# Graph layer and expert layer on one core: order of stored groups, earlier YTh, YTl and YL, and a last group finished by tiles

## The chip, the cores and the metric

The kernel runs on one core of one Trainium2 chip. The metric is device time in microseconds: the median over runs of the whole program. Each run is one launch.

## The reference

There are 12,500 nodes with 256 values each and 200,000 edges. Two layers follow each other, both with a residual:

```python
x = x + gnn(layernorm(x), src, dst, edge_weight, W, b)      # segment_sum((X @ W)[src] * w, dst) + b
x = x + ffn(layernorm(x)[None], Wr, br, W1, b1, W2, b2, gamma, beta)[0]

# ffn, with xn = layernorm(x), 8 experts, D = 256, F = 512
logits = mean(xn over nodes) @ Wr + br                      # one routing for all nodes
two experts with the largest weight, softmax over these two # only known when every node is done
h = gelu(xn @ W1[e] + b1[e]);  y[e] = h @ W2[e] + b2[e]
out = layer_norm(sum_e weight[e] * y[e] + xn) * gamma + beta
```

The routing needs the mean over all nodes, so the two experts are known only when the graph layer has ended.

## The kernel before, in words

The 98 tiles of 128 nodes are processed in 25 groups: group 0 has two tiles, the others four. Groups 0 to 7 (`AHEAD = 8`) are put through all eight experts during the graph layer, while TensorE has room, and their outputs are stored in DRAM (`y_d`); they are called stored groups here. Groups 8 to 24, the list `post` of 17 groups, are put through the two chosen experts in a last stage. The change lies in that last stage alone.

The last stage computes in split precision. An fp32 value is written as a rounded part and the rest: YTh and YTl for the turned input of a group, W1h and W1l, W2h and W2l for the weights, Hhi and Hlo for the hidden values. Three products replace one.

All engines run their instructions in the order in which the program writes them, and wait on semaphores. The loops of the last stage go over rounds `k` and steps `i` of 0 to 7 (`HID = 8`), a step being 128 of the 2 x 512 hidden columns:

- **TensorE**: round `k` does `up(k+1, i)`, then `down(k, i)`. `up` needs YTh (L1463) and YTl (L1466) of its group, and that Hhi of four steps earlier has been made (four PSUM banks). `down(k, i)` needs Hlo of that step; twelve products (L1494) of four tiles, and at the last step two bias matmuls (L1499).
- **ScalarE**: round `k` does `hidden(k, i)`, two Gelu passes (Ht, L878, and Hhi, L881); the results of TensorE's round `k - 1` come to it step by step. In between stand `high(k+1)` (YTh, L804) at step 3, and `normal2(n)` (XN, L812), which needs XL in SBUF: at step 4 for a stored group, at step 6 for group `k`.
- **VectorE**: round `k` does `low_h(k, i)` (Hlo, L1194), and in between `low(k+1)` (YTl, L1105) at step 4, and the finishing of group `post[k-2]`: `total` at steps 0 and 1 (add L1211, statistics L1219, aggregation L1222, variance L1225) and `give` at steps 3 and 4 (L1232, L1237). Where `k - 2` is a key of `pre_of`, a stored group is finished too, at steps 2, 5 and 7; such a round is called a doubled round.
- **GpSimd**: adds a bias to XN of stored groups (L576), adds beta to XL (L578), and raises the variance to the power -0.5 (ZR, L583) for each group.
- **SyncE** issues all DMAs of the stage in one order, `for n, g in enumerate(order)`: for a group of `post` first `load_yl(k+3)`, then it waits until the group is finished (`s_fin`), stores it, loads XL of the fourth group after it, and after a stored group the next stored outputs (YP).

`order` puts the stored groups between those of `post`: `pre_of` maps a place in `post` to the stored group that follows it. Before, the places are 1, 2, 4, 6, 8, 9, 11 and 13, so VectorE's doubled rounds are 3, 4, 6, 8, 10, 11, 13 and 15. VectorE's loop runs two rounds longer than TensorE's, and finishes the last two groups there.

Of the kernel before, what the change touches and what calls it, by code (L numbers as in the profile page):

```python
# [4 lines left out]
P = 128  # L5
NODES, D, F, E = 12500, 256, 512, 8
# [100 lines left out]
def gnn_ffn(nc, x, dflat, srct, dstt, wt, W, b, Wr, br, W1, b1t, W2, b2, gamma, beta, cst, iota_e, evt, out):  # L107
# [13 lines left out]
    with ctx:  # L121
# [5 lines left out]
        def sem(name):  # L127
            return ctx.enter_context(nc.semaphore(name))
# [122 lines left out]
        s_xbn, s_xag, s_xv, s_xy, s_xq, s_xs = sem("dve_x_stats"), sem("dve_x_aggr"), sem("dve_x_var"), sem("act_x_seed"), sem("dve_x_newton"), sem("act_x_scale")  # L251
# [109 lines left out]
        def _(e):  # L361
# [147 lines left out]
            e.wait_ge(s_w2l, 2)  # L509
            for a in range(2):  # L510
                load_y(a)
            k = 0
            for n, g in enumerate(order):
                m = len(tiles(g))
                if g >= AHEAD:
                    if k + 3 < len(post):
                        load_yl(k + 3)
                    k += 1
                e.wait_ge(s_fin, first_of[n] + m)
                top = NT - tiles(g)[0] - m  # L520
                if g == 0:
                    e.dma_start(out[top * P:(NT - 1) * P, :].rearrange("(t p) d -> p t d", p=P), Z[:, n % 3, 0:m - 1, :]).then_inc(out_st[n % 3], 16)
                    e.dma_start(out[(NT - 1) * P:NODES, :], Z[0:LAST, n % 3, m - 1, :]).then_inc(out_last, 16)
                else:
                    e.dma_start(out[top * P:(top + m) * P, :].rearrange("(t p) d -> p t d", p=P), Z[:, n % 3, 0:m, :]).then_inc(out_st[n % 3], 16)
                if n + 4 < NG:
                    load_x1(n + 4)
                if g + 2 < AHEAD:
                    load_y(g + 2)
            for k in range(3):  # L530
                e.wait_ge(out_st[k], 16 * ((NG - 1 - k) // 3 + 1))
            e.wait_ge(out_last, 16)

        @block.gpsimd
        def _(e):
# [50 lines left out]
            for n in range(NG):  # L586
                until = min(n + (2 if n + 1 < NG and order[n + 1] < AHEAD else 1), NG - 1)
                while added <= until:
                    add_rows(added)
                    added += 1  # L590
                rstd(n)

        @block.scalar
        def _(e):
# [168 lines left out]
            def seed_x(b):  # L763
                a, z = lots[b][0] * GT, min(lots[b][-1] * GT + GT, NT)
                e.wait_ge(s_xv, b + 1)
                e.activation(xy[:, a:z], xv[:, a:z], ACT.Abs_reciprocal_sqrt).then_inc(s_xy, 1)

            def scale_x(b):
                e.wait_ge(s_xq, 3 * b + 3)
# [114 lines left out]
            for k in range(len(post) + 1):  # L884
                for i in range(HID):
                    if k < len(post):
                        hidden(k, i)
                    if k == 0 and i in (2, 3):
                        high_w2(i - 2)
                    if i == 3 and 1 <= k and k + 1 < len(post):  # L890
                        high(k + 1)
                    if i == 1 and k == 1 or i == 4 and k - 1 in pre_of:
                        normal2(n)
                        n += 1
                    if i == 6 and 1 <= k < len(post):
                        normal2(n)
                        n += 1
            assert n == NG

        @block.vector  # L900
        def _(e):
# [45 lines left out]

            def x_newton(b):
                a, z = lots[b][0] * GT, min(lots[b][-1] * GT + GT, NT)
                e.wait_ge(s_xy, b + 1)  # L950
                e.tensor_tensor(out=xq[:, a:z], in0=xy[:, a:z], in1=xy[:, a:z], op=ALU.mult).then_inc(s_xq, 1)
                e.wait_ge(s_xq, 3 * b + 1)
                e.scalar_tensor_tensor(out=xq[:, a:z], in0=xq[:, a:z], scalar=-0.5, in1=xv[:, a:z], op0=ALU.mult, op1=ALU.mult).then_inc(s_xq, 1)
                e.wait_ge(s_xq, 3 * b + 2)
                e.scalar_tensor_tensor(out=xr[:, a:z], in0=xq[:, a:z], scalar=1.5, in1=xy[:, a:z], op0=ALU.add, op1=ALU.mult).then_inc(s_xq, 1)

            e.wait_ge(dst_in, 32)
            e.tensor_scalar(LOW[:, :], DST[:, :], P - 1, None, ALU.bitwise_and).then_inc(s_tab, 1)
# [282 lines left out]
                e.wait_ge(x1_st[k], 16 * ((NT - 1 - k) // 4 + 1))  # L1241
            for k in range(2):
                e.wait_ge(ye_st[k], 16 * (UNITS // 2))
            for k in range(len(post) + 2):
                n = place[post[k - 2]] if k >= 2 else None
                two = k - 2 in pre_of
                for i in range(HID):
                    if k < len(post):
                        low_h(k, i)
                    if k == 0 and i in (2, 4):  # L1250
                        low_w2(i // 2 - 1)
                    if k == 0 and i == 7:
# [10 lines left out]
                        give(n, slice(2, 4))  # L1263
                    if two and i == 5:
                        total(n + 1, None, slice(2, 4))
                    if i == 4 and 1 <= k and k + 1 < len(post):
                        low(k + 1)
                    if two and i == 7:
                        give(n + 1, slice(0, 4))

        @block.tensor
        def _(e):
# [280 lines left out]
```

## Time and profile before

| | |
|---|---|
| median of 3 runs | 2426.01 us (2422.8 to 2431.03) |
| profiled execution | 2431.56 us |
| its span | 2429.8 us |
| busy: TensorE, VectorE, ScalarE, GpSimd | 2240.1, 1025.5, 1184.3, 1618.5 us |
| mean granted clock of TensorE | 0.972 |
| the last stage (first `down` to the end) | from 2027.1 to 2429.8 us of the span |

Everything in front of 2020 us of the span is the sorting tables, the graph layer and the stored groups, and the diff leaves its instructions as they are. A busy share for the whole span says little about the last stage; it is read by windows and by the timeline of each engine. Idle time of an engine other than TensorE costs nothing there as long as TensorE goes on.

### The profile page before, as it was taken

How to read it: one execution, taken by the hardware profiler on the slowest of the kernel's cores; microseconds unless marked ns; L12 is line 12 of the kernel's file. 1: busy time of each engine (PE TensorE's matmuls, PEld its weight loads, DVE VectorE, ACT ScalarE, POOL GpSimd, SP SyncE). 2: the span in 40 equal slices, each digit the busy share in tenths (PEclk: the TensorE clock that was granted, in tenths of full speed). 3: DMA queues.
4: the chain of work that ended last, by engine and by line, in shares of the span. 5: the costliest groups of instructions: out<-in, count | busy, mean ns of one | idle time of the engine just before them, and what ended most of it. 6: DMA issues, size and time to landing. Idle time of an engine off the chain costs nothing. (4 is left out here: it accounts for less than half of the span.)

```text
span 2429.8 us, 41873 instructions
## 1 busy us (share of the span) xinstructions
PE 2240.1 (92%) x9976; PEld 1736.3 (71%) x9977; DVE 1025.5 (42%) x2959; ACT 1184.3 (49%) x3197; POOL 1618.5 (67%) x1628
## 2 busy tenths in 40 slices
PE   2488999899999999999999999999998999999997
PEld 1366777676776767777776777777776788998887
DVE  7883223222232223222322323232321246888897
ACT  3577666665665555545434343332323117556463
POOL 6677777777777777777777777777777741324241
PEclk8699999999999999999999999999999999999999
DMA  9855667666665555566556555565565533233321
GB/s 371 317 171 156 201 200 235 188 184 181 180 186 179 179 170 174 176 183 192 185 172 186 186 182 183 181 182 176 177 193 164 182 115 105 100 131 113 122 96 53
DMA packets 226708, 425.79 MB, mean 175 GB/s; under 512 B 36643, under 2 KB 134742, under 8 KB 226568
## 3 DMA queue, kind: packets, MB, share of 16 engines
q0 software_dynamic: 75008, 204.90, 28.1%
q1 hardware_dynamic: 151128, 217.12, 27.3%
q10 hardware_dynamic: 432, 2.40, 0.3%
q14 instruction: 113, 0.93, 0.1%
q8 instruction: 27, 0.44, 0.1%
HBM read 341.53 MB, written 82.75 MB: 175 GB/s over the span
## 5 line engine op out<-in xcount | busy, mean ns | idle before, releaser
L559 POOL DMA_INDIRECT G<-xr_d,SRC x1467 | 1396.7, 952 | 447.2 <-issue 295.1
L1053 DVE TENSOR_SCALAR OH<-CST,DL,WR 128x128 f32<-128x128 f32 x1564 | 563.9, 368 | 1296.7 <-PE ps L1374 1151.6
L1374 PE MATMUL ps<-G,OH 128*128 x3128 | 751.2, 394 | 92.5 <-DVE OH L1053 53.0
L1374 PEld LDWEIGHTS ps<-G,OH 128*128 128x128 f32 x3128 | 599.6, 196 | 257.2 <-issue 179.6
L1346 PE MATMUL ps<-YU,W1u 128*128 128x512 f32 (+1 forms) x1024 | 426.3, 569 | 8.5 <-ACT H L753 7.3
L1357 PE MATMUL ps<-W2u,H 128*128 128x256 f32 x1920 | 428.6, 381 | 4.9 <-issue 4.4
L1357 PEld LDWEIGHTS ps<-W2u,H 128*128 128x128 f32 x1920 | 361.4, 190 | 66.9 <-issue 19.4
L1346 PEld LDWEIGHTS ps<-YU,W1u 128*128 128x128 f32 x1024 | 195.0, 191 | 205.0 <-issue 184.9
L761 ACT ACTIVATE YE<-ps 128x512 f32<-128x512 f32 (+1 forms) x128 | 72.7, 570 | 462.7 <-PE ps L1357 462.7
L753 ACT ACTIVATE H<-ps,b1a 128x512 f32<-128x512 f32 (+1 forms) x256 | 168.6, 661 | 225.9 <-PE ps L1346 225.7
L638 ACT ACTIVATE OHX<-OHT,WR 128x128 f32<-128x128 f32 x194 | 67.2, 394 | 231.7 <-PE ps L1374 231.7
L583 POOL TENSOR_TENSOR ZR<-ZV,mhalf 128x4 f32<-128x4 f32 (+1 forms) x25 | 33.4, 1335 | 191.2 <-DVE ZV L1225 191.2
L1494 PE MATMUL ps<-W2h,Hlo 128*128 128x256 f32 x544 | 154.2, 283 | 0.0
L1494 PE MATMUL ps<-W2l,Hhi 128*128 128x256 f32 x544 | 154.1, 283 | 0.0
L1494 PE MATMUL ps<-W2h,Hhi 128*128 128x256 f32 x544 | 153.6, 282 | 0.0
L1194 DVE TENSOR_TENSOR Hlo<-Ht,Hhi 128x512 fp32r<-128x512 f32 x136 | 127.3, 950 | 59.5 <-ACT Hhi L881 59.3
L878 ACT ACTIVATE Ht<-ps,b1s 128x512 f32<-128x512 f32 x136 | 93.7, 689 | 100.0 <-PE ps L1473 100.0
L559 POOL DMA_INDIRECT G<-in_x,SRC x96 | 93.0, 969 | 45.4 <-issue 24.4
L1494 PEld LDWEIGHTS ps<-W2h,Hhi 128*128 128x128 f32 x544 | 104.3, 192 | 5.6
L1494 PEld LDWEIGHTS ps<-W2l,Hhi 128*128 128x128 f32 x544 | 104.2, 192 | 5.1
L1325 PE MATMUL ps<-Wsb,AT 128*128 128x256 f32 x412 | 106.9, 382 | 0.0
L1494 PEld LDWEIGHTS ps<-W2h,Hlo 128*128 128x128 f32 x544 | 104.1, 191 | 0.0
(206 smaller groups left out, 2330.4 us busy)
## 6 DMA issues: line engine op xcount, KB each, us to landing
W1u<-in_W SPq DMA_DIRECT2D x64, 512.0 KB
W2u<-in_W SPq DMA_DIRECT2D x64, 512.0 KB, 4.7
y_d<-YE SPq DMA_DIRECT2D x56, 512.0 KB, 5.4
G<-xr_d,SRC POOLq DMA_INDIRECT x1467, 2.9
x_d<-X SPq DMA_DIRECT2D x98, 128.0 KB, 2.1
yt_d<-YT SPq DMA_DIRECT2D x98, 128.0 KB, 2.5
XR<-in_x SPq DMA_DIRECT2D x97, 128.0 KB, 3.1
XS<-in_x SPq DMA_DIRECT2D x24, 512.0 KB, 19.3
```

Of the source, the lines that this page charges most:

```text
L559: e.indirect_dma_start(out=G[0:rows(s), s % RING, :], out_offset=None, in_=x if s < FRESH else xr_d, in_offset=bass.IndirectOffsetOnAxis(a ...
L638: e.activation(OHX[:, k, :], OHT[:, 1, k, :], ACT.Copy, scale=WR[:, bass.ds(odd + k, 1)]).then_inc(s_ohx, 1)
L753: e.activation(H[:, i, 0:w], ps[:, UP[i % 2], 0:w], ACT.Gelu, bias=b1a[:, u % E, i:i + 1]).then_inc(s_gelu, 1)
L761: e.activation(YE[:, u % 2, p * w:(p + 1) * w], ps[:, DN[p], 0:w], ACT.Copy).then_inc(s_ye, 1)
L878: e.activation(Ht[:, i % HB, 0:w], ps[:, 4 + i % HB, 0:w], ACT.Gelu, bias=b1s[:, i // 4, i % 4:i % 4 + 1]).then_inc(s_ht, 1)
L1053: e.tensor_scalar(OH[:, s % OHR, :], iota, DL[:, s:s + 1], WR[:, s + 1:s + 2], ALU.is_equal, ALU.mult).then_inc(s_oh, 1)
L1194: e.tensor_tensor(out=Hlo[:, h, 0:w], in0=Ht[:, i % HB, 0:w], in1=Hhi[:, h, 0:w].bitcast(f32), op=ALU.subtract).then_inc(s_hlo, 1)
L1325: e.matmul(ps[:, XB, 0:D], AT[:, c * P:(c + 1) * P], Wsb[:, c, :], start=False, stop=True, skip_group_check=True)
L1346: ins = e.matmul(ps[:, UP[i % 2], 0:m * P], W1u[:, c, i * P:(i + 1) * P], YU[:, c, 0:m * P], start=(c == 0), stop=(c == 1))
L1357: ins = e.matmul(ps[:, DN[p], h * D:(h + 1) * D], H[:, i, j * P:(j + 1) * P], W2u[:, i, :], start=(h == 0 and i == 0), stop=(i == 3), skip ...
L1374: e.matmul(ps[:, 0, 0:D], OH[:, r, :], Gf[:, bass.ds(g + r * D, D)], start=False, stop=True, skip_group_check=True).then_inc(s_main, 1)
L1494: ins = e.matmul(acc, hp[:, h, rows], wp[:, x_, f, :], start=(i == 0 and q % 2 == 0 and a == 0), stop=False, skip_group_check=True)
```

## The change

Five things are changed.

1. `pre_of` becomes 0, 1, 3, 5, 7, 9, 11, 13: the doubled rounds of VectorE are 2, 3, 5, 7, 9, 11, 13 and 15.
2. ScalarE makes YTh at step 1 of a round in place of step 3, VectorE makes YTl at step 2 in place of step 4.
3. YL, which both read, is loaded one group sooner: `load_yl(3)` ahead of the loop, `load_yl(k + 4)` in it.
4. The last round of `down` is written out: all steps for tiles 0 and 1, then all steps for tile 2, then for tile 3 in PSUM bank 4, each with a bias matmul and a semaphore of its own. The last two groups are finished in four parts (`PARTS`): the last group but one, tiles 0 and 1 of the last, tile 2, tile 3, and the last group is stored by three DMAs.
5. For these parts GpSimd's power goes: ScalarE gives a seed with `Abs_reciprocal_sqrt`, for which it first loads another function table, and VectorE does a Newton step in three small operations.

```diff
-        pre_of = {1 + (len(post) - 3) * a // AHEAD: a for a in range(AHEAD)}
+        pre_of = {max(0, 2 * a - 1): a for a in range(AHEAD)}
...
+        PARTS = ((NG - 2, slice(0, len(tiles(order[NG - 2])))), (NG - 1, slice(0, 2)), (NG - 1, slice(2, 3)), (NG - 1, slice(3, 4)))
...
+            load_yl(3)
...
-                    if k + 3 < len(post):
-                        load_yl(k + 3)
+                    if k + 4 < len(post):
+                        load_yl(k + 4)
...
+                elif n == NG - 1:
+                    for _, some in PARTS[1:]:
+                        e.wait_ge(s_fin, first_of[n] + some.stop)
+                        e.dma_start(out[(top + some.start) * P:(top + some.stop) * P, :].rearrange("(t p) d -> p t d", p=P), Z[:, n % 3, some, :]).then_inc(out_st[n % 3], 16)
...
-                rstd(n)
+                if n < NG - 2:
+                    rstd(n)
...
-                    if i == 3 and 1 <= k and k + 1 < len(post):
+                    if i == 1 and 1 <= k and k + 1 < len(post):
                         high(k + 1)
...
+            e.activation(r1[:, 6:7], eps[:, 0:1], ACT.Abs_reciprocal_sqrt)
+            for j, (n, some) in enumerate(PARTS):
+                e.wait_ge(s_zv, NG - 2 + j + 1)
+                e.activation(ZR[:, n % 3, some], ZV[:, n % 3, some], ACT.Abs_reciprocal_sqrt).then_inc(s_seed, 1)
...
-            for k in range(len(post) + 2):
+            def finish(j):
...
+                m, b = len(qs), len(lots) + j
+                e.wait_ge(s_seed, b + 1)
+                e.tensor_tensor(out=RA[:, 0:m], in0=ZR[:, n % 3, some], in1=ZR[:, n % 3, some], op=ALU.mult).then_inc(s_newton, 1)
+                e.wait_ge(s_newton, 3 * b + 1)
+                e.scalar_tensor_tensor(out=RA[:, 0:m], in0=RA[:, 0:m], scalar=-0.5, in1=ZV[:, n % 3, some], op0=ALU.mult, op1=ALU.mult).then_inc(s_newton, 1)
+                e.wait_ge(s_newton, 3 * b + 2)
+                e.scalar_tensor_tensor(out=ZR[:, n % 3, some], in0=RA[:, 0:m], scalar=1.5, in1=ZR[:, n % 3, some], op0=ALU.add, op1=ALU.mult).then_inc(s_newton, 1)
...
+            for k in range(len(post)):
...
+                    if i == 2 and 1 <= k and k + 1 < len(post):
+                        low(k + 1)
...
-                    if i == 4 and 1 <= k and k + 1 < len(post):
-                        low(k + 1)
...
+            for j in range(len(PARTS)):
+                finish(j)
...
+            k = len(post) - 1
+            e.wait_ge(s_z, first_of[NG - 3] + len(tiles(order[NG - 3])))
+            for i in range(HID):
+                e.wait_ge(s_hlo, HID * k + i + 1)
+                for q in range(2):
+                    ins = products(ps[:, 2 * (k % 2), q * D:(q + 1) * D], k, i, q, i == 0 and q == 0)
...
+            for q, acc in ((2, ps[:, 2 * (k % 2) + 1, 0:D]), (3, ps[:, 4, 0:D])):
+                for i in range(HID):
+                    products(acc, k, i, q, i == 0)
+                e.matmul(acc, ones_r[:, :], B2r[:, 0, :], start=False, stop=True, skip_group_check=True).then_inc(s_pdn, 1)
```

The program also renames two semaphores (`s_xy`, `s_xq` become `s_seed`, `s_newton`).

The instructions on VectorE in its round 10, from step 1 to step 4, before; L1214 and L1216 are the two sums of a stored group, L1194 is a step's Hlo:

```order
L1194 TENSOR_TENSOR Hlo<-Ht,Hhi 128x512
L1211 TENSOR_TENSOR Z<-ps,XN 128x256 x2
L1219 BN_STATS ZST<-Z 128x6 x2
L1222 BN_AGGR ZMV<-ZST 128x2 x2
L1225 TENSOR_SCALAR ZV<-ZMV 128x4
L1194 TENSOR_TENSOR Hlo<-Ht,Hhi 128x512
L1214 SCALAR_TENSOR_TENSOR Z<-YP_126,r,XN 128x256
L1216 SCALAR_TENSOR_TENSOR Z<-YP_126,r,Z 128x256
```

And with the change, the same steps of the same round; Hlo is L1208, the add L1225, the variance L1239, YTl L1119:

```order
L1208 TENSOR_TENSOR Hlo<-Ht,Hhi 128x512
L1225 TENSOR_TENSOR Z<-ps,XN 128x256 x2
L1233 BN_STATS ZST<-Z 128x6 x2
L1236 BN_AGGR ZMV<-ZST 128x2 x2
L1239 TENSOR_SCALAR ZV<-ZMV 128x4
L1208 TENSOR_TENSOR Hlo<-Ht,Hhi 128x512
L1119 TENSOR_TENSOR YTl<-YL,YTh 128x512 x2
L1208 TENSOR_TENSOR Hlo<-Ht,Hhi 128x512
```

The stored group has left this round, and YTl stands behind the third Hlo, where the sums of the stored group stood.

VectorE's queue at its very end, before, from the add of the last group on:

```order
L1211 TENSOR_TENSOR Z<-ps,XN 128x256 x2
L1219 BN_STATS ZST<-Z 128x6 x2
L1222 BN_AGGR ZMV<-ZST 128x2 x2
L1225 TENSOR_SCALAR ZV<-ZMV 128x4
L1232 SCALAR_TENSOR_TENSOR Z<-Z,ZMV,g_bc 128x256 x2
L1237 SCALAR_TENSOR_TENSOR Z<-Z,ZR,XL 128x256 x2
```

And with the change, its last part, which is tile 3 alone:

```order
L1267 TENSOR_TENSOR Z<-ps,XN 128x256
L1270 BN_STATS ZST<-Z 128x6
L1273 BN_AGGR ZMV<-ZST 128x2
L1275 TENSOR_SCALAR ZV<-ZMV 128x1
L1278 SCALAR_TENSOR_TENSOR Z<-Z,ZMV,g_bc 128x256
L1281 TENSOR_TENSOR RA<-ZR 128x1
L1283 SCALAR_TENSOR_TENSOR RA<-RA,ZV 128x1
L1285 SCALAR_TENSOR_TENSOR ZR<-RA,ZR 128x1
L1290 SCALAR_TENSOR_TENSOR Z<-Z,ZR,XL 128x256
```

The same operations now stand once a tile, with three Newton operations between L1278 and L1290.

## Rows read from the trace of the kernel before

**Rows 1.** The page: its first row.

```profile
span 2429.8 us, 41873 instructions
```

**Rows 2.** Windows: stretch, us, busy PE, PEld, DVE, ACT, POOL, clock, DMA, GB/s.

```profile
2050.10:2142.20 92.10, 92.10 (x585) 83.53 (x585) 71.36 (x162) 54.47 (x95) 27.73 (x14) 1.00 0.30 101
...
2259.80:2290.20 30.40, 24.87 (x148) 21.56 (x147) 25.33 (x56) 15.69 (x28) 10.52 (x5) 0.91 0.35 118
...
2320.00:2366.00 46.00, 46.00 (x294) 41.73 (x293) 43.47 (x88) 27.68 (x48) 18.29 (x8) 1.00 0.29 92
```

**Rows 3.** Waits of TensorE from 2020 us, and one row of its timeline.

```profile
PE ps L1466 <- DVE YTl L1105: 4.4, 4, 2.3
...
2284.85 1.19 PE L1463 MATMUL ps<-YTh,W1h 128*128 128x512 f32 x2 [3.25 <-issue]
```

**Rows 4.** The chain that ended last: start us, us, what.

```profile
2337.46 1.43 PE ps L1494 x12
...
2360.47 1.43 PE ps L1494 x12
```

**Rows 5.** Timeline of TensorE: first products of two rounds.

```profile
2142.20 0.28 PE L1494 MATMUL ps<-W2h,Hhi 128*128 128x256 f32 x1
...
2314.29 0.28 PE L1494 MATMUL ps<-W2h,Hhi 128*128 128x256 f32 x1
```

**Rows 6.** Timelines of ScalarE, VectorE and SyncE, 2261 to 2284 us.

```profile
2261.34 1.09 ACT L812 ACTIVATE XN<-XL,NR,R 128x256 f32<-128x256 f32 x2 [6.18 <-DMA XL<-x_d]
...
2265.36 5.97 DVE L1232 SCALAR_TENSOR_TENSOR Z<-Z,ZMV,g_bc 128x256 f32<-128x256 f32 x4
...
2275.45 0.43 SPq L505 DMA_DIRECT2D YL<-yt_d  x1
...
2282.45 1.15 ACT L804 ACTIVATE YTh<-YL 128x512 fp32r<-128x512 f32 x2 [12.72 <-DMA YL<-yt_d]
```

**Rows 7.** Timelines of ScalarE, VectorE and SyncE at the end.

```profile
2404.14 0.67 ACT L881 ACTIVATE Hhi<-ps,b1s 128x512 fp32r<-128x512 f32 x1
...
2406.62 0.74 DVE L1211 TENSOR_TENSOR Z<-ps,XN 128x256 f32<-128x256 f32 x2
...
2417.23 0.76 DVE L1211 TENSOR_TENSOR Z<-ps,XN 128x256 f32<-128x256 f32 x2 [3.45 <-PE ps L1499]
...
2421.93 0.88 DVE L1237 SCALAR_TENSOR_TENSOR Z<-Z,ZR,XL 128x256 f32<-128x256 f32 x2 [0.56 <-DVE Z L1232]
...
2423.52 0.88 DVE L1237 SCALAR_TENSOR_TENSOR Z<-Z,ZR,XL 128x256 f32<-128x256 f32 x2
...
2413.81 10.99 SPq L525 DMA_DIRECT2D out<-Z  x2
```

**Rows 8.** Groups by line and shape: busy us, mean ns, idle before.

```profile
L1237 DVE SCALAR_TENSOR_TENSOR Z<-Z,ZR,XL 128x256 f32<-128x256 f32 x98 | 43.2, 487 | 1.1 <-DVE Z L1232 1.1
L1219 DVE BATCH_NORM_STATS2 ZST<-Z 128x6 f32<-128x256 f32 x98 | 36.3, 412 | 0.0
L1211 DVE TENSOR_TENSOR Z<-ps,XN 128x256 f32<-128x256 f32 x68 | 25.3, 412 | 3.4 <-PE ps L1499 3.4
L1222 DVE BATCH_NORM_AGGREGATE ZMV<-ZST 128x2 f32<-128x6 f32 x98 | 14.6, 172 | 0.0
```

**Rows 9.** Timelines of ScalarE and VectorE: seed, Newton operations, table load.

```profile
91.82 0.19 ACT L766 ACTIVATE xy<-xv 128x6 f32<-128x6 f32 x1
...
92.04 0.17 DVE L951 TENSOR_TENSOR xq<-xy 128x6 f32<-128x6 f32 x1 [1.30 <-ACT xy L766]
...
92.44 0.17 DVE L955 SCALAR_TENSOR_TENSOR xr<-xq,xy 128x6 f32<-128x6 f32 x1
...
2014.89 1.28 ACT L858 ACT_TABLE_LOAD   x1
```

**Rows 10.** DMA issues: what, count, KB each, us to landing.

```profile
out<-Z SPq DMA_DIRECT2D x3, 512.0 KB, 2.9
...
out<-Z SPq DMA_DIRECT2D x1, 128.0 KB, 1.7
```

More of the change, by code:

```diff
@@ L267, in gnn_ffn @@
         post = list(range(AHEAD, NG))
-        pre_of = {1 + (len(post) - 3) * a // AHEAD: a for a in range(AHEAD)}
+        pre_of = {max(0, 2 * a - 1): a for a in range(AHEAD)}
+        assert len(pre_of) == AHEAD and max(pre_of) <= len(post) - 4
         order = [n for k, g in enumerate(post) for n in ((g, pre_of[k]) if k in pre_of else (g,))]
@@ L281, in gnn_ffn @@
         s_zr, s_zg, s_fin, s_b1s = sem("pool_zr"), sem("dve_zg"), sem("dve_fin"), sem("dve_b1")
+        PARTS = ((NG - 2, slice(0, len(tiles(order[NG - 2])))), (NG - 1, slice(0, 2)), (NG - 1, slice(2, 3)), (NG - 1, slice(3, 4)))
+        assert order[NG - 2:] == [NG - 2, NG - 1] and len(tiles(NG - 1)) == 4
         out_st, out_last = [sem(f"out{k}") for k in range(3)], sem("out_last")
@@ L515, in _ @@
                 if g >= AHEAD:
-                    if k + 3 < len(post):
-                        load_yl(k + 3)
+                    if k + 4 < len(post):
+                        load_yl(k + 4)
                     k += 1
-                e.wait_ge(s_fin, first_of[n] + m)
+                if n < NG - 1:
+                    e.wait_ge(s_fin, first_of[n] + m)
                 top = NT - tiles(g)[0] - m
@@ L765, in seed_x @@
                 e.wait_ge(s_xv, b + 1)
-                e.activation(xy[:, a:z], xv[:, a:z], ACT.Abs_reciprocal_sqrt).then_inc(s_xy, 1)
+                e.activation(xy[:, a:z], xv[:, a:z], ACT.Abs_reciprocal_sqrt).then_inc(s_seed, 1)
             def scale_x(b):
-                e.wait_ge(s_xq, 3 * b + 3)
+                e.wait_ge(s_newton, 3 * b + 3)
                 for g in lots[b]:
@@ L949, in x_newton @@
                 a, z = lots[b][0] * GT, min(lots[b][-1] * GT + GT, NT)
[L950 to L955, printed above, removed]
+                e.wait_ge(s_seed, b + 1)
+                e.tensor_tensor(out=xq[:, a:z], in0=xy[:, a:z], in1=xy[:, a:z], op=ALU.mult).then_inc(s_newton, 1)
+                e.wait_ge(s_newton, 3 * b + 1)
+                e.scalar_tensor_tensor(out=xq[:, a:z], in0=xq[:, a:z], scalar=-0.5, in1=xv[:, a:z], op0=ALU.mult, op1=ALU.mult).then_inc(s_newton, 1)
+                e.wait_ge(s_newton, 3 * b + 2)
+                e.scalar_tensor_tensor(out=xr[:, a:z], in0=xq[:, a:z], scalar=1.5, in1=xy[:, a:z], op0=ALU.add, op1=ALU.mult).then_inc(s_newton, 1)
             e.wait_ge(dst_in, 32)
@@ L1508, in _, with products @@
                 up(0, i)
-            for k in range(len(post)):
+            def products(acc, k, i, q, start):
+                x_, f, h = i // 4, i % 4, k % 2 * HID + i
+                rows = slice((GT - 1 - q) * P, (GT - q) * P)
+                for a, (hp, wp) in enumerate(((Hhi, W2h), (Hhi, W2l), (Hlo, W2h))):
+                    ins = e.matmul(acc, hp[:, h, rows], wp[:, x_, f, :], start=(start and a == 0), stop=False, skip_group_check=True)
+                return ins
+            for k in range(len(post) - 1):
                 for i in range(HID):
-                    if k + 1 < len(post):
-                        up(k + 1, i)
+                    up(k + 1, i)
                     down(k, i)
+            k = len(post) - 1
[4 more added lines that the diff above has]
+                    ins = products(ps[:, 2 * (k % 2), q * D:(q + 1) * D], k, i, q, i == 0 and q == 0)
+                if i == HID - 1:
+                    ins = e.matmul(ps[:, 2 * (k % 2), :], ones_r[:, :], B2r[:, :, :].rearrange("p c d -> p (c d)"), start=False, stop=True, skip_group_check=True)
+                ins.then_inc(s_pdn, 1)
+            for q, acc in ((2, ps[:, 2 * (k % 2) + 1, 0:D]), (3, ps[:, 4, 0:D])):
+                for i in range(HID):
+                    products(acc, k, i, q, i == 0)
+                e.matmul(acc, ones_r[:, :], B2r[:, 0, :], start=False, stop=True, skip_group_check=True).then_inc(s_pdn, 1)
 def kernel(**inputs):
```

35 lines of the change are left out of this document (31 added, 4 removed).

## The prediction, made before the change was run

> **What bounds the kernel now.** I read the page first for the span [rows 1], then the windows of the last stage, cut at the rounds of TensorE. A round is eight steps of `up(k+1, i)` and `down(k, i)`. TensorE is busy for all of the 92.1 us of its rounds 1 to 4, and for all of 46.0 us further on, at the full granted clock (1.00, which is 2.4 GHz). In the 30.4 us from `down(10, 0)` to `down(11, 0)` it is busy for 24.87 and the mean clock is 0.91 [rows 2]. So this stage is bound by TensorE, except where it pauses. The waits say for what: 4.4 us in four pauses for VectorE's YTl, and 3.25 us in front of L1463 at 2284.85, the matmul that reads YTh and also needs an Hhi that stands behind YTh in ScalarE's queue [rows 3]. The chain of waits gives an undisturbed round: `down(13, 0)` starts at 2337.46 and `down(14, 0)` at 2360.47, so 23.01 us [rows 4]. From the first matmul of `down(5, 0)` at 2142.20 to that of `down(12, 0)` at 2314.29 are 172.09 us [rows 5], where seven rounds need 7 x 23.01 = 161.07. The pauses, with the half clock behind the longest, thus cost 11.0 us. That is more than the 7.7 us waited, because TensorE computes part of that stretch at its lower level (1.2 GHz, which gives the mean of 0.91).
>
> Why it pauses is a loop through four queues, in time order [rows 6]. ScalarE waits 6.18 us for XL before it normalizes a group in round 10, with the rest of `hidden` queued behind it. VectorE can finish its stored group only afterwards, and four L1232 take 5.97 us there, because GpSimd adds to XL at the same time. SyncE sits on that group's `s_fin`, so the load of YL is issued at 2275.45. ScalarE waits 12.72 us for it, and makes YTh only at 2282.45. YTl comes after that, and `up(12, 0)` needs both. The same queue order makes the two smaller pauses.
>
> At the end nothing of TensorE is left to hide under. VectorE begins with the last group but one at 2406.62, then idles 3.45 us for the last matmul, begins the last group at 2417.23, idles another 0.56 us for GpSimd's inverse deviations, and starts its last pair of L1237 at 2423.52. The output DMA of 512 KB is issued at the end of the SyncE row that runs to 2424.80, and the span ends at 2429.8 [rows 1, 7].
>
> **The change part by part.** *YL a group sooner.* No DMA is added: `load_yl(k+4)` stands where `load_yl(k+3)` stood. Its wait, s_ytl >= 2k+6, is met at step 2 of VectorE's round k+1, and SyncE comes past no earlier than step 4 of that round, so SyncE isn't held. YL then has a full round (23.0 us) more, of which the earlier YTh below uses 5.6. The longest lateness to cover is the 12.72 us that ScalarE waited [rows 6]; 4.7 us of margin stay. Value taken: no wait for YL is left.
>
> *YTh at step 1, YTl at step 2.* The same instructions, two steps sooner. A step is an eighth of 23.01, about 2.8 us; so YTh and YTl come 5.6 us sooner before `up(k+1, 0)`. What is queued behind them moves back by the same instruction time that is taken away further down. Cost: nothing, hidden under TensorE.
>
> *Stored groups in every other round.* Before, they were finished in VectorE's rounds 3, 4, 6, 8, 10, 11, 13 and 15; after, in 2, 3, 5, 7, 9, 11, 13 and 15. The pair 10, 11, with the 5.97 us row in it, is gone. A new pair, 2 and 3, takes the place of 3 and 4. The rhythm of alternate rounds exists already from 2320 to 2366: VectorE is busy for 43.47 of 46.0 us and TensorE for all 46.0 [rows 2]. The pair 3, 4 lies in the 92.1 us stretch without a pause [rows 2], and the stored group of round 2 is half a group. So I take the cost as nothing. With the two steps above this stage gives back all of the 11.0 us. Bounds: 11.0, and 3.6 if the new pair costs as much as the largest pause, 30.4 - 23.0 = 7.4 us [rows 2].
>
> *Last group by tiles.* TensorE does 96 products as before and three bias matmuls, of 512, 256 and 256 columns, in place of two of 512: the same columns. Twelve products take 1.43 us [rows 4], so all of it 8 x 1.43 + 0.5 = 11.9, back from 2417.2 [rows 7]: it starts at 2405.3. The first two tiles are ready near 2411.2, the third near 2414.2, the fourth at 2417.2. VectorE has it all to do from 2406.62 [rows 7]. The add, the statistics, the aggregation and L1237 take 0.41, 0.41, 0.17 and 0.49 us for a tile [rows 8]. Back to back they start sooner: two adds take 0.74, so the second starts 0.33 after the first, and two L1237 take 0.88, so 0.40 apart [rows 7]; I take 0.33 for the statistics and 0.40 for L1232 too. The Newton steps start 0.20 apart (92.04 to 92.44 for two), so three cost 0.6; the seed on ScalarE takes 0.19 us and VectorE goes on 0.03 after it [rows 9].
> - last group but one: 4 x 0.33 + 4 x 0.33 + 0.55 + 0.08 + 4 x 0.40 + 0.6 + 4 x 0.40 = 7.1, to 2413.7;
> - tiles 0 and 1: 0.67 + 0.66 + 0.34 + 0.08 + 0.8 + 0.6 + 0.8 = 3.95, to 2417.7. They were ready at 2411.2: the idle 3.45 us are filled;
> - tile 2, alone, each operation waiting for the one before: 0.45 + 0.45 + 0.21 + 0.53 (L1232 beside the seed) + 0.6 + 0.40 = 2.65, to 2420.35;
> - tile 3: the same up to the start of its last operation, 2.25, and 0.48 for this: ends at 2423.1.
>
> Before, the last L1237 ended at 2423.52 + 0.88 = 2424.4: 1.3 us saved. The last DMA now has 128 KB: such a store of Z landed in 1.7 us, those of 512 KB in 2.9 [rows 10]: 1.2 us. Together 2.5. ScalarE's other table is loaded in 1.28 us [rows 9] after its last Hhi, which ends at 2404.8 [rows 7]; that is 2406.1, and the first seed is wanted near 2410. It is hidden by VectorE's sums, and would cost up to 1.3 if ScalarE came 4 us later. Bounds of the tail: if no two operations overlapped, the sums with whole durations (0.41, 0.41, 0.17, 0.49, 0.49 a tile, and 0.17 per small one) are 8.6 + 4.6 + 2 x 2.65 = 18.5, to 2425.1, and the gain is 1.2 - 0.7 = 0.5. On the other side each seed could be hidden altogether (0.1 each less): 2.7.
>
> The Trainium skill states such a rule in "VectorE: DVE Perf Modes", section The DRAIN you can't avoid: the next operation starts only when the pipe of the one before is empty. By it splitting the tail into parts would pay every length in full, the 0.5 us bound. The rows disagree with it where operations don't depend on each other: two L1237 take 0.88 us [rows 7], not twice their mean.
>
> **Sum.** 11.0 + 2.5 = 13.5 us. The profiled execution took 2431.56 us, so it would take 2418.1. The median of the runs is 2426.01, 5.55 us lower; taken from that, **2412.5 us**. Anything within 0.3% (7.3 us) can't be told from no change in a measurement of this kernel.
>
> **The rivals.**
> *The tail gives nothing (0.10).* The gain there is the 0.5 of the bound: 11.5 us, 2414.5. For it: tiles 2 and 3 are chains without overlap. Against it: even so VectorE fills 3.45 idle us [rows 7].
>
> *The pauses were larger in the profiled execution (0.10).* All 5.55 us by which it is above the median could be pauses of this stage, since these hang on when DMAs land. Then the median gains 13.5 - 5.55 = 7.95: 2418.1. Against it: the gathers in front of this stage, over four fifths of the span, can vary as well.
>
> *The pause moves to the new pair (0.10).* XL of the fifth group in order is loaded after the first is finished, at step 4 of round 2, and ScalarE wants it at step 6. That is the pattern that made it wait 6.18 us [rows 6]. GpSimd's adds for the stored group fall there too. Against it: the 6.18 us end at 2261.3, and TensorE's first pause after them ends at 2284.85, behind YL [rows 3, 6]; they made none of their own, and YL no longer hangs on them. If it isn't covered, it costs up to 7.4: 2419.9, half that 2416.2.
>
> *VectorE becomes the bound, slower (0.05).* In alternate rounds it has 46.0 - 43.47 = 2.5 us left in two rounds [rows 2], and there are six such pairs of rounds after. A collision with GpSimd costs 5.97 - 2 x 0.88 = 4.2 us [rows 6, 7]. One more in each pair costs 6 x 1.7 = 10 us (2422.7, no change); from two on it decides: 6 x (8.4 - 2.5) = 35, so 2448. Against it: these collisions are already in the 43.47.
> In the Trainium skill, "GPSIMD Engine Reference", section Key points, GpSimd contends with those VectorE instructions that have two SBUF inputs or a two-port mode. The 5.97 us row agrees with that. By that rule every move of VectorE's sums beside GpSimd's adds is a risk, and this change moves them.
>
> **How the numbers follow.** Forecast 0.65, the others as given. The forecast's own spread is 2409 to 2416, from the bounds of the tail and the scatter of the runs. The range 2408 to 2419 takes in the tail, the smaller pauses and half of the moved pause, and leaves out slower, the worst of the moved pause and a part on either side, under 0.2. Faster by over 0.3%: 0.65 + 0.10 + half of 0.10 + half of 0.10 = 0.85; within 0.3%: 0.10; slower 0.05.
>
> **What would show it.** Right: `down(k, 0)` starts every 23.0 us from round 0 to 16; TensorE has no pause on YTl or YTh and clock 1.00 throughout; ScalarE waits for no YL; VectorE doesn't idle from the last Hlo to the end; the last store is 128 KB and lands in under 2 us. Wrong: a pause of TensorE in rounds 1 to 4 (moved), pauses on Hhi or Hlo in rounds 5 to 15 (VectorE bound), or idle time in front of the Newton steps of the last tiles, or a table load that ends after VectorE's first ZV.

## The result, and the profile after the change

| | before | changed |
|---|---|---|
| median, on the same chip | 2429.43 us (6 runs, 2422.8 to 2431.38) | 2410.81 us (6 runs, 2407.87 to 2415.06) |
| ratio | | 0.9932, 95% interval 0.9917 to 0.9947: 0.7% faster |
| profiled execution | 2431.56 us | 2415.06 us |
| its span, mean clock | 2429.8 us, 0.972 | 2413.3 us, 0.985 |

The forecast was 2412.5 us, 1.7 us above the median that was measured. That it came so near is in part luck. The gain between the medians is 18.6 us where the sum said 13.5, and the forecast was taken from a median of 2426.01 us (3 runs), where six runs of the same kernel give 2429.43: 3.4 us of the missing 5.1 were made up by that. The two medians lie 2.1 us further apart than the profiled executions, which is less than the runs of either kernel differ among themselves. The two profiled executions are 16.5 us apart, and the last stage can be divided so that each part of these 16.5 us is seen. The dividing points are the first products of round 0 and round 15 of `down`. First the two rows of the timeline of TensorE before, then the two of the changed kernel (start us, us, instruction):

```profile
2027.14 0.28 PE L1494 MATMUL ps<-W2h,Hhi 128*128 128x256 f32 x1
...
2383.32 0.28 PE L1494 MATMUL ps<-W2h,Hhi 128*128 128x256 f32 x1
```

```profile
2026.62 0.28 PE L1543 MATMUL ps<-W2h,Hhi 128*128 128x256 f32 x1
...
2371.82 0.28 PE L1543 MATMUL ps<-W2h,Hhi 128*128 128x256 f32 x1
```

| stretch | before | changed | difference |
|---|---|---|---|
| to round 0 of `down` | 2027.14 | 2026.62 | 0.5, scatter of the part that is not changed |
| round 0 to round 15 | 356.18 | 345.20 | 11.0 |
| round 15 to the end of the span | 46.44 | 41.44 | 5.0 |

The spans end at 2429.76 and 2413.26 us; the views round this to 0.1 us. A fifteenth of 345.20 is 23.01 us: a round lasts now what [rows 4] showed for an undisturbed one. The windows of the changed kernel say it again (columns as in [rows 2]):

```profile
2055.00:2370.00 315.00, 315.00 (x2003) 285.87 (x2003) 281.47 (x604) 190.85 (x330) 97.41 (x50) 1.00 0.33 110
```

TensorE is busy for all of the 315 us at clock 1.00, and VectorE for 281.47 of them. In the waits of the same stretch (us in total, times, longest) TensorE has no row, and ScalarE none for YL:

```profile
ACT Ht L888 <- PE ps L1522: 111.8, 81, 1.7
DVE Hlo L1208 <- ACT Hhi L891: 30.3, 32, 7.3
...
ACT XN L822 <- DMA XL<-x_d: 7.4, 1, 7.4
ACT Ht L888 <- DVE Hlo L1208: 5.0, 2, 4.1
```

At the end, the timeline of VectorE, which answers to [rows 7]:

```profile
2393.35 1.85 DVE L1208 TENSOR_TENSOR Hlo<-Ht,Hhi 128x512 fp32r<-128x512 f32 x1 [2.41 <-ACT Hhi L891]
2395.12 1.40 DVE L1267 TENSOR_TENSOR Z<-ps,XN 128x256 f32<-128x256 f32 x4
2396.45 1.39 DVE L1270 BATCH_NORM_STATS2 ZST<-Z 128x6 f32<-128x256 f32 x4
...
2401.98 0.74 DVE L1267 TENSOR_TENSOR Z<-ps,XN 128x256 f32<-128x256 f32 x2
...
2405.89 0.41 DVE L1267 TENSOR_TENSOR Z<-ps,XN 128x256 f32<-128x256 f32 x1
2406.34 0.43 DVE L1270 BATCH_NORM_STATS2 ZST<-Z 128x6 f32<-128x256 f32 x1
...
2408.46 0.42 DVE L1267 TENSOR_TENSOR Z<-ps,XN 128x256 f32<-128x256 f32 x1
...
2410.62 0.48 DVE L1290 SCALAR_TENSOR_TENSOR Z<-Z,ZR,XL 128x256 f32<-128x256 f32 x1
```

The rows of ScalarE and GpSimd beside it:

```profile
2393.33 1.28 ACT L909 ACT_TABLE_LOAD   x1
...
2398.35 0.20 ACT L912 ACTIVATE ZR<-ZV 128x4 f32<-128x4 f32 x1 [3.52 <-DVE ZV L1275]
...
2392.25 2.39 POOL L587 TENSOR_TENSOR XL<-XL,be_bc 128x1024 f32<-128x1024 f32 x1 [10.29 <-ACT XN L822]
```

None of VectorE's finishing rows has idle time in front. VectorE ends at 2410.62 + 0.48 = 2411.10, that is 39.3 us after the start of round 15, where it ended 41.1 after it before (2423.52 + 0.88 - 2383.32, [rows 7]): 1.8 us. The other 3.2 of the 5.0 us lie behind VectorE's last instruction: from there to the end of the span it was 2429.76 - 2424.40 = 5.4 us, and is 2413.26 - 2411.11 = 2.2 us (2411.10 by the row). The store that is smaller now explains 1.2 of them. The other 2.0 are seen in the instructions that every engine's queue runs at the end of the program, which the profile puts under one line, L121 (engine, operation, how often: shortest/median/longest ns, first and last start). Before:

```profile
L121 POOLq DRAIN  x1: 8907/8907/8907, 2420.6 to 2420.6; - x1
...
L121 SPq DRAIN  x1: 7/7/7, 2427.5 to 2427.5; - x1
```

Changed:

```profile
L121 POOLq DRAIN  x1: 10119/10119/10119, 2392.2 to 2392.2; - x1
...
L121 SPq DRAIN  x1: 7/7/7, 2413.0 to 2413.0; - x1
```

Before, SyncE had seen the last store land and closed at 2427.5, and GpSimd's DRAIN, which it issues when it has nothing left but its last power, ran on to 2420.6 + 8.9 = 2429.5. In the changed kernel the same instruction begins at 2392.2, and its 10.1 us are over at 2402.3, 0.3 us after VectorE has begun the last group and 8.8 us before it ends.

### The profile page after: what moved, and what is told of

It reads as the page before. It is cut to its first block and busy times, and to the rows that moved or that the text cites. A ratio compares the mean times of both kernels' runs of the same rounds, so it can differ in the third digit from the quotient of the medians.

```text
span 2413.3 us, 41880 instructions
## 1 busy us (share of the span) xinstructions
PE 2236.1 (93%) x9977; PEld 1734.3 (72%) x9978; DVE 1024.2 (42%) x2973; ACT 1188.6 (49%) x3203; POOL 1597.6 (66%) x1626
## 5 line engine op out<-in xcount | busy, mean ns | idle before, releaser
L1208 DVE TENSOR_TENSOR Hlo<-Ht,Hhi 128x512 fp32r<-128x512 f32 x136 | 125.1, 927 | 50.9 <-ACT Hhi L891 50.4
L1543 PE MATMUL ps<-W2h,Hlo 128*128 128x256 f32 x512 | 144.9, 283 | 0.0
L1543 PE MATMUL ps<-W2l,Hhi 128*128 128x256 f32 x512 | 144.8, 283 | 0.0
L1543 PE MATMUL ps<-W2h,Hhi 128*128 128x256 f32 x512 | 144.2, 282 | 0.0
L1543 PEld LDWEIGHTS ps<-W2h,Hhi 128*128 128x128 f32 x512 | 97.8, 191 | 5.5
L1543 PEld LDWEIGHTS ps<-W2l,Hhi 128*128 128x128 f32 x512 | 97.8, 191 | 5.0
L1543 PEld LDWEIGHTS ps<-W2h,Hlo 128*128 128x128 f32 x512 | 97.8, 191 | 0.0
```

The costliest lines, as they stand in the source:

```text
L1208: e.tensor_tensor(out=Hlo[:, h, 0:w], in0=Ht[:, i % HB, 0:w], in1=Hhi[:, h, 0:w].bitcast(f32), op=ALU.subtract).then_inc(s_hlo, 1)
L1543: ins = e.matmul(acc, hp[:, h, rows], wp[:, x_, f, :], start=(i == 0 and q % 2 == 0 and a == 0), stop=False, skip_group_check=True)
```

## Experiments

e1 to e8 ran where the kernel before took 3277 to 3279 us: there the part in front of the last stage lasts some 850 us longer, and the whole times of one kernel scatter by up to 27 us. A last stage without pauses is the same there to 0.02 us (345.18 and 345.20), so the experiments are told by these stretches, as above, and the whole times only where a kernel was timed in rounds (e1, e2, e8, e9). Each stretch is read from one execution. The pauses themselves are less steady: the stage of before took 357.29 us there (e2) and 356.18 above, so what is said of pauses holds to about 1 us. "Behind VectorE" is from the end of VectorE's last instruction to the end of the span.

| kernel | round 0 to 15 | round 15 to end | VectorE's end after the start of round 15 | behind VectorE |
|---|---|---|---|---|
| before | 356.18 | 46.4 | 41.1 | 5.4 |
| changed | 345.20 | 41.4 | 39.3 | 2.2 |
| e1, stage alone | 345.18 | 46.4 | 41.1 | 5.4 |
| e2, tail alone | 357.29 | 41.4 | 39.3 | 2.1 |
| e3, order alone | 352.0 | 46.4 | | |
| e4, YL alone | 352.06 | 46.4 | | |
| e10, YTh and YTl alone | 394.56 | 46.4 | | |
| e7, YL, YTh, YTl, old order | 345.20 | 46.4 | | |
| e11, YL and order | 345.18 | 46.4 | | |
| e5, no tiles | 345.18 | 44.2 | 40.9 | 3.4 |
| e6, late power | 345.18 | 46.7 | 39.3 | 7.4 |
| e8, pairs | 345.18 | 40.3 | 38.1 | 2.2 |
| e9, pairs and XN sooner | 345.20 | 39.7 | 37.5 | 2.3 |

**e1, the stage without the tail.** The kernel before with the parts 1, 2 and 3 of the change.

```diff
-        pre_of = {1 + (len(post) - 3) * a // AHEAD: a for a in range(AHEAD)}
+        pre_of = {max(0, 2 * a - 1): a for a in range(AHEAD)}
...
-                        load_yl(k + 3)
+                        load_yl(k + 4)
...
-                    if i == 3 and 1 <= k and k + 1 < len(post):
+                    if i == 1 and 1 <= k and k + 1 < len(post):
```

> The kernel before with the new order of stored groups, the earlier YTh and YTl and the earlier YL, but its own last round and its own finish of the last two groups. My theory: it holds all of the pauses' 11.0 us, down(k,0) every 23.0 us from round 0 to 16, and the time from the start of down(15) to the end stays at the 46.5 us of before: about 11 us below before. Rival, that the tail gave more than the 2.5 us I put on it because something beside VectorE's work and the last DMA ends there: the rest of the change's 16.5 us, so 5.0 to 5.5 us, is missing here, and GpSimd's end (its last power) closes the program later than the last DMA lands.

Median 3263.72 us against 3277.02, ratio 0.9968 (0.9951 to 0.9986). All of the 11 us between the rounds come back, and nothing at the end.

**e2, the tail without the stage.** The changed kernel with these edits taken back.

> The changed kernel with the order, YTh, YTl and YL of before; only the last round by tiles, the four parts and the Newton steps. The pauses of before stay (11.0 us up to down(15)). My prediction's tail of 2.5 us is too small if this run is 5 us below before; the rival that this surplus belongs to the scatter in front of the stage would leave 2.5 us.

Median 3271.72 us, ratio 0.9978 (0.9963 to 0.9994). The tail is worth 5.0 us whatever lies in front of it, and the two halves add up.

**e3 and e4, one edit each.** The kernel before with the new `pre_of` alone (e3), or with YL a group sooner alone (e4).

> The kernel before with only the new order of stored groups. If the doubled pair 10 and 11 is the whole cause, all pauses go (11.0 us). If the load of YL behind the stored group's finish is the cause, the 7.4 us behind the pair go, but each doubled round that also loads YP (5, 7, 9, 11) pays a pause of 1.0 to 1.5 us as rounds 6 and 8 do before: 4 to 6 us of pauses stay, and the doubled rounds 13 and 15, which load no YP, pay none.

> The kernel before with only YL loaded a group sooner; the doubled pair 10 and 11 stays, with ScalarE's wait of some 6 us for XL. If YL is the cause, all pauses go (11.0 us) and ScalarE waits for no YL. If the pair is, the pause at the start of round 11 stays at several us.

Neither gives all: 4.2 and 4.1 us of the 11.0 (5.3 and 5.2, if taken from the 357.29 us of e2, which ran beside them). So of each pair of expectations neither came alone: with the order alone 7.0 us of pauses stay, in rounds 5, 6, 9 and 11, where the second expectation had 4 to 6; with YL alone 5.1 us stay in round 11, and 1.7 in the next. With the order alone ScalarE still waits 42.8 us for YL, in seven waits, and TensorE for YTl in three (waits from 2905 to 3240 us):

```profile
ACT YTh L804 <- DMA YL<-yt_d: 42.8, 7, 8.4
...
PE ps L1466 <- DVE YTl L1105: 4.4, 3, 1.9
```

With YL alone ScalarE has no such wait, and TensorE stands once for YTl. Its row, and VectorE's timeline in front of it:

```profile
3144.88 1.22 PE L1467 MATMUL ps<-YTl,W1h 128*128 128x512 f32 x2 [3.95 <-DVE YTl L1106]
```

```profile
3133.24 3.02 DVE L1233 SCALAR_TENSOR_TENSOR Z<-Z,ZMV,g_bc 128x256 f32<-128x256 f32 x2
3136.18 3.02 DVE L1238 SCALAR_TENSOR_TENSOR Z<-Z,ZR,XL 128x256 f32<-128x256 f32 x2
3139.12 2.92 DVE L1195 TENSOR_TENSOR Hlo<-Ht,Hhi 128x512 fp32r<-128x512 f32 x1
3141.96 0.87 DVE L1233 SCALAR_TENSOR_TENSOR Z<-Z,ZMV,g_bc 128x256 f32<-128x256 f32 x2
...
3143.55 1.28 DVE L1106 TENSOR_TENSOR YTl<-YL,YTh 128x512 fp32r<-128x512 f32 x2
```

YTl at step 4 stands behind the end of two doubled rounds, in which operations of 0.87 us take 3.02 and an Hlo of 0.69 takes 2.92. Three adds of GpSimd lie beside these rows:

```profile
3133.57 2.41 POOL L577 TENSOR_TENSOR XN<-XN,B 128x1024 f32<-128x1024 f32 x1
3135.93 2.59 POOL L579 TENSOR_TENSOR XL<-XL,be_bc 128x1024 f32<-128x1024 f32 x1
3139.09 2.41 POOL L579 TENSOR_TENSOR XL<-XL,be_bc 128x1024 f32<-128x1024 f32 x1 [0.57 <-ACT XN L813]
```

They make the three rows 2 x 2.15 + 2.23 = 6.5 us longer, more than the 3.95 us that TensorE waits. So there were two causes, one after the other: YL late, and behind it VectorE late with YTl, by the doubled pair and by GpSimd's adds in it. No run takes these two apart.

**e7, the old order with everything else of the stage.** The edits of e1 without `pre_of`.

> The kernel before with YTh, YTl and YL sooner, and the old order of stored groups, so VectorE has doubled rounds 10 and 11 in a row. Start of round 0 to start of round 15 of down: 356.19 us before, 345.18 with all three edits of the stage, 352.06 with YL alone. Theory: the order only mattered because YTl at step 4 stood behind the work of two doubled rounds; at step 2 it is in time, so 345.2 to 346.2 us, and the new order was needless. Rival: two doubled rounds in a row are more work for VectorE than two rounds of TensorE last, so that Hlo or YTl is late whatever their step: at least 2 us more than 345.2, with the pause in rounds 11 to 13.

345.20 us. The two doubled rounds 10 and 11 are harmless once YTl doesn't stand behind them: VectorE is busy 286.96 of 315 us, and TensorE all 315.

**e11, the new order and YL, with YTh and YTl at their old steps.**

> The kernel before with the new order and YL a group sooner, YTh and YTl at their old steps 3 and 4, and the old tail. Theory: with YL there in time, only the pair of doubled rounds 10 and 11 still made YTl late (352.06 us with YL alone); without a pair YTl at step 4 is in time, so no pause is left: 345.2 to 345.5 us from round 0 to round 15. Rival: a single doubled round is already enough to make YTl at step 4 late: pauses of 0.1 to 1.5 us in each of the rounds behind a doubled one, 346 to 350 us; the new pair of doubled rounds 2 and 3 alone could cost up to 5 us at round 3 or 4.

345.18 us: no pause either, not even behind the new pair 2 and 3. With YL sooner, the order and the earlier steps are two ways to do the same thing. The third pair, the order and the earlier steps without YL, was not run.

**e10, YTh and YTl sooner, nothing else.**

```diff
-                    if i == 3 and 1 <= k and k + 1 < len(post):
+                    if i == 1 and 1 <= k and k + 1 < len(post):
                         high(k + 1)
...
-                    if i == 4 and 1 <= k and k + 1 < len(post):
-                        low(k + 1)
```

> The kernel before with only YTh (step 1 in place of 3) and YTl (step 2 in place of 4) sooner; the old order, YL as before, and the old tail. Round 0 to round 15 of down: 356.19 before, 352.0 with the order alone, 352.06 with YL alone, 345.20 with YL, YTh and YTl. Theory: YL itself lands too late behind the stored groups' stores, so ScalarE and VectorE reach their YTh and YTl steps and wait for it; part of the pauses stays, 348 to 353 us, with ScalarE waiting for YL. Rival: the steps were all that mattered: 345.2 us, and YL sooner was needless.

Both expectations failed: 394.56 us, 38.4 more than before (2464.13 us in all). ScalarE waits for YL in twelve places, by the waits from 2055 to 2462 us:

```profile
ACT YTh L804 <- DMA YL<-yt_d: 115.0, 12, 15.3
```

Its timeline shows two of them; SyncE's rows between stand behind:

```profile
2108.42 1.15 ACT L804 ACTIVATE YTh<-YL 128x512 fp32r<-128x512 f32 x2 [9.92 <-DMA YL<-yt_d]
...
2139.82 1.15 ACT L804 ACTIVATE YTh<-YL 128x512 fp32r<-128x512 f32 x2 [15.29 <-DMA YL<-yt_d]
```

```profile
2129.79 0.39 SPq L525 DMA_DIRECT2D out<-Z  x1
2130.22 0.51 SPq L475 DMA_DIRECT2D XL<-x_d  x1
...
2132.31 0.43 SPq L505 DMA_DIRECT2D YL<-yt_d  x1
```

ScalarE stands at step 1 of its round, waiting for YL with the Gelu passes of steps 2 to 7 queued behind it. Without them VectorE gets no Hhi: in the first of the two waits it idles 6.61 us:

```profile
2110.75 0.69 DVE L1194 TENSOR_TENSOR Hlo<-Ht,Hhi 128x512 fp32r<-128x512 f32 x1 [6.61 <-ACT Hhi L881]
```

From then on it has no idle time until its stored group is finished, at 2129.76. SyncE stands at that group's store, and YL is issued behind it, at 2132.31; ScalarE has it at 2139.82, in the second wait. So one wait for YL makes VectorE late with a finish, and that finish makes the next YL late. The loop of [rows 6] feeds itself when YTh is wanted two steps sooner. Seven of the 15 rounds are longer for it, by 1.4 to 12.3 us each. The chain is read from these rows. What was tested is its remedy: e7, which is this kernel with YL a group sooner, has no pause.

**e5, no tiles.** The changed kernel with the last group in one part and one store and TensorE's last round in its old form, Newton step and seed kept.

```diff
-        PARTS = ((NG - 2, ...), (NG - 1, slice(0, 2)), (NG - 1, slice(2, 3)), (NG - 1, slice(3, 4)))
+        PARTS = ((NG - 2, ...), (NG - 1, slice(0, 4)))
```

> The changed kernel with the last group finished whole, in one part, from sums made as before, and stored by one DMA; the seed on ScalarE and the Newton step on VectorE stay for the last two groups, so GpSimd has nothing to do at the end. From the start of the sixteenth round of down (round 15) to the end it was 46.44 us before and 41.44 us changed. Theory: before, the program could not end until GpSimd, whose last power began at 2420.66, had finished its closing DRAIN of 8.9 us; without a late power the end comes as soon as the last store has landed. VectorE then ends 41.08 + 0.6 (Newton) = 41.7 us after that start, and the end follows 3.4 us later (from before: end of VectorE to landing of the 512 KB store and SyncE's own close): 45.1 us. Rival: the 5.40 us between VectorE's end and the program's end are the price of a 512 KB store and its close, whatever GpSimd does: 41.7 + 5.4 = 47.1 us. Second rival: all of the 5.0 us come from finishing by tiles: 46.4 to 47.1 us as well.

44.2 us, where the theory said 45.1 and the rivals 46.4 to 47.1. Without a late power on GpSimd, 3.4 us are left behind VectorE's end in place of 5.4, as the theory said. The 0.9 us are VectorE's: it ends 0.2 us sooner than before, where I had added 0.6 for the three Newton operations. They take the place of the idle 0.56 us for the power [rows 7].

**e6, a power that nobody reads.**

```diff
+            e.wait_ge(s_zv, NG + 2)
+            e.tensor_tensor(out=ZR[:, (NG - 3) % 3, 0:1], in0=ZV[:, (NG - 1) % 3, 3:4], in1=mhalf[:, 0:1], op=ALU.pow).then_inc(s_zr, 1)
```

> The changed kernel with one more instruction on GpSimd: a power of one column, started by the variance of the last tile, whose result nobody reads. Theory (GpSimd's closing DRAIN): the last variance stands 3.4 us before the program's end, so the power starts 3.3 us before it, and with 1.2 us for it and 8.9 us of DRAIN the program ends 6.8 us later: 48.2 us from the start of round 15 of down to the end, in place of 41.44. Rival (the end is set by the last store alone): 41.44 us, no change, since no work depends on the power. A third outcome, 0.5 to 2 us more, would mean that the power only disturbs VectorE's last instructions.

46.7 us, 5.2 more than without it. The timeline of GpSimd shows the power, and the instructions under L121 what follows:

```profile
3248.05 0.73 POOL L603 TENSOR_TENSOR ZR<-ZV,mhalf 128x1 f32<-128x1 f32 x1 [15.19 <-DVE ZV L1277]
```

```profile
L121 POOLq DRAIN  x1: 8456/8456/8456, 3248.0 to 3248.0; - x1
...
L121 SPq DRAIN  x1: 7/7/7, 3251.3 to 3251.3; - x1
```

VectorE ends as in the changed kernel (39.3 us after the start of round 15), SyncE closes as there, and then the program waits 5.2 us for GpSimd. The theory's 48.2 was 1.5 too much, mostly because I added the DRAIN to the end of the power; it is issued with the power, and its length includes it. From the end of GpSimd's last instruction to the end of the DRAIN it is 7.7 us in all three traces: before 2420.62 + 8.91 - (2420.66 + 1.18), changed 2392.21 + 10.12 - (2392.25 + 2.39), and here 3248.02 + 8.46 - (3248.05 + 0.73). The traces of the other ten kernels give the same 7.69 us.

**e8, pairs.** The last two tiles in one part, stored one by one.

```diff
-        PARTS = (..., (NG - 1, slice(0, 2)), (NG - 1, slice(2, 3)), (NG - 1, slice(3, 4)))
+        PARTS = (..., (NG - 1, slice(0, 2)), (NG - 1, slice(2, 4)))
```

> The changed kernel with tiles 2 and 3 of the last group finished in one part, in pairs of instructions, still stored by a DMA each; TensorE's part is as in the changed kernel. VectorE reaches the third part at 2405.9 us of the changed kernel's span, and TensorE's last matmul for tile 3 ends near 2405.4, so both tiles are there. Two tiles take 3.91 us (2401.98 to 2405.89), two single ones 2.57 and 2.64. Theory: the tail is VectorE's, so its end comes 1.3 us sooner: 40.1 us from the start of round 15 to the end in place of 41.44. Rival 1: the sums of tile 3 are not ready and VectorE waits, 0 to 1.3 us given back. Rival 2: two stores issued 0.4 us apart get in each other's way and the last lands later, 0.3 to 0.6 us given back.

40.3 us, 1.1 less than the changed kernel; VectorE's end came 1.2 sooner. Against before the ratio was 0.9954 (0.9932 to 0.9976).

**e9, pairs, and the last group's XN two steps sooner.**

```diff
-                    if i == 1 and k == 1 or i == 4 and k - 1 in pre_of:
+                    if i == 1 and k == 1 or i == 4 and (k - 1 in pre_of or k == len(post) - 1):
```

> The kernel with pairs (its last stage from round 15 of down to the end: 40.32 us), and in round 16 ScalarE makes the last group's XN at step 4 in place of step 6, so that GpSimd's add to XL, 2.39 us long and begun at 2392.25 in the changed kernel, is over before the last Hlo, which lasted 1.85 us beside it where the one before it lasted 0.69. Theory: VectorE's finish starts when the last Hlo ends (2395.12), though the sums of round 15 are there near 2393.7 (TensorE goes on to round 16 without a pause), so it starts 1.2 us sooner; the third part then waits some 0.4 us for the sums of tile 3. VectorE's end and the program's end come 0.8 us sooner: 39.5 us. Rival: the finish starts when TensorE's sums are there and the slow Hlo was hidden: 40.3 us, no change. Rival 2: at step 4 the same add slows other Hlo passes or Hhi comes late, TensorE waits in its last round and the sums of tile 3 come later: 40.3 us or more.

39.7 us, 0.6 less than e8, where the theory said 39.5. It ran on a chip where before took 2430.85 us: 2413.02 us, ratio 0.9927 (0.9914 to 0.9941). Its timeline of VectorE:

```profile
2395.39 0.69 DVE L1208 TENSOR_TENSOR Hlo<-Ht,Hhi 128x512 fp32r<-128x512 f32 x1 [2.13 <-ACT Hhi L891]
2396.09 1.42 DVE L1267 TENSOR_TENSOR Z<-ps,XN 128x256 f32<-128x256 f32 x4
...
2406.87 0.42 DVE L1267 TENSOR_TENSOR Z<-ps,XN 128x256 f32<-128x256 f32 x1
2407.96 0.42 DVE L1267 TENSOR_TENSOR Z<-ps,XN 128x256 f32<-128x256 f32 x1 [0.68 <-PE ps L1581]
```

The last Hlo takes 0.69 us where it took 1.85 beside GpSimd's add, and the finish starts 21.9 us after the start of round 15 in place of 23.3. The add now lies beside an Hlo of two steps earlier, which takes 1.98 us (at 2390.03), and that one has idle time behind it. Of these 1.4 us 0.8 are given back: VectorE now reaches tile 3 before TensorE has summed it, and waits 0.68. From here on the tail is TensorE's as well. The 1.7 us of e9 over the changed kernel are read from the stretches; the ratios to before overlap and can't tell the two kernels apart.

## Why the prediction was right, and where its sum was not

**The pauses: as predicted.** 11.0 us were forecast and 11.0 came (e1: 356.18 to 345.18). `down(k, 0)` starts every 23.0 us, ScalarE waits for no YL, the clock is 1.00. This term was a difference of two measured lengths, seven rounds with the pauses in them and without, and so had the price of the half clock in it.

**YL a group sooner: right, and more than I said.** Neither of the other two edits alone brings YL in time: ScalarE still waits for it in seven places with the new order (e3), and in twelve with the earlier steps (e10). Whether both together would do was not run. In the changed kernel's records, from round 2 on YL had landed at least 8.4 us before ScalarE wanted it, and I had 4.7 of margin. In the kernel before it was there last, with ScalarE waiting, for 7 of the 17 groups.

**The order and the earlier steps: either, not both.** I explained the gain by the three edits together, and didn't ask what each does alone. e7 and e11 show that behind YL either of the others is enough. "Cost: nothing, hidden under TensorE" for the earlier YTh and YTl holds only because YL comes sooner: e10 costs 38.4 us. My working had the reason in it (5.6 of YL's 23.0 us are used by the earlier YTh), but not the sign without it.

**The tail: right in its mechanism, mis-sized.** "2.5 us", with 2.7 as the upper bound, measured 5.0. By its parts:
- VectorE: 1.3 predicted, 1.8 measured. The chain of a single tile took 2.57 us (2405.89 to 2408.46) for my 2.65, and the last group but one 6.86 for 7.1; the rest are hundredths of the same kind.
- the smaller store: 1.2 predicted, 1.2 measured (e5 against the changed kernel, 3.4 and 2.2 behind VectorE).
- the power taken from GpSimd: counted only as a price of the Newton step. It gave 2.0 us (e5, 5.4 and 3.4 behind VectorE), since GpSimd's close of the program no longer comes last. e6 shows the mechanism from the other side.

The step that failed is the one from VectorE's end to the end of the span. I took the change there to be that of the store's landing alone. My own rows spoke against it: the store was issued by 2424.80 [rows 7] and lands in 2.9 us [rows 10], so it was there by 2427.7, while the span ends at 2429.8 [rows 1]. These 2.1 us had no owner in the prediction. That made the upper bound of the tail too low, and the sum with it: 13.5 for 16.5 between the profiled executions, of which 2.5 are the tail's and 0.5 the scatter in front of the stage. The forecast of 2412.5 hides this, since the median that it started from was 3.4 us low.

**The table load and VectorE's idle time: as predicted.** The load is over at 2394.6, and the first seed is wanted at 2398.35; VectorE has no idle time from its last Hlo to its end.

**The rivals.** *The tail gives nothing* fell: it gives 5.0. Its ground was that operations don't overlap. By the rule of the Trainium skill ("VectorE: DVE Perf Modes", The DRAIN you can't avoid) the four adds at 2395.12 would last four full lengths, 1.65 us; the row says 1.40, and the next operation starts 1.33 after them. The section itself says that a next operation that isn't held starts earlier, and the four adds, with no wait between them, bear that out. For a single tile, where each operation needs the one before, the starts lie 0.45 us apart (2405.89, 2406.34), a little over a whole length. So there the rule's price holds. *The pauses were larger in the profiled execution*: nothing speaks for it. e2, in another execution and on another chip, has 357.29 us for the same code, 1.1 more and not up to 5.55 less, and the medians gained more than the profiled executions. The pauses of the executions that weren't profiled are not known. *The pause moves to the new pair*: the pattern came about, ScalarE waited 7.4 us for XL in round 2, and TensorE lost nothing. *VectorE becomes the bound* fell: it idles 30.3 us in 32 waits for Hhi in the 315 us.

## What to carry to other kernels

- From the last instruction of the busiest engine to the end of the span, name the owner of each microsecond: issue, landing, and each engine's closing instructions. An engine off the path can end the program; here it was GpSimd, by one power of four columns. Give an engine with a long close its last instruction early.
- Before moving an instruction that waits for a transfer, ask which work the transfer itself waits for through other queues; moved ahead of that work, it can hold up its own input. The earlier YTh and YTl were worth nothing with YL and the order changed (e11, e1), 6.9 us with YL alone changed (e4, e7), and minus 38 us with neither (e10). So test the parts of a change apart before crediting one.
- A price taken as the difference of two measured lengths, with and without the pause, was right to 0.1 us; the one put together from parts had one part missing.

## What the runs showed of the hardware that was not expected

- GpSimd's DRAIN at the end of the program ends 7.69 us after its last instruction, in all thirteen traces, whether that is a power of one or four columns or an add of 1024. The closing DRAINs of VectorE, ScalarE, TensorE and SyncE last 0.8, 1.6, 2.6 and 0.01 us in the trace of before.
- GpSimd's add beside VectorE: the last Hlo took 1.85 us beside it and 0.69 without (e9), and in e4 operations of 0.87 us took 3.02. The add itself takes 2.39 to 2.59 us. The Trainium skill ("GPSIMD Engine Reference", Key points) says that GpSimd contends with VectorE instructions that have two SBUF inputs; both kinds of rows here have two, and agree.
- The part in front of the last stage took some 850 us longer on one chip than on the other, with the same instructions, and the last stage, where it had no pauses, did not change by more than 0.02 us (345.18 and 345.20); with the pauses of before it was 1.1 us longer there (357.29 and 356.18). What slows it there was not examined.
